# The mixed tile's column sums: written by ScalarE in row order to a gate buffer's free half, and read contiguously by the merge

## The reference, cut to what matters

```
def cross_scan(x):                       # x: image with 192 channels
    x0 = x.reshape(B, -1, L)             # position r*48+c  (row order)
    x1 = jnp.swapaxes(x, 2, 3).reshape(B, -1, L)   # position c*48+r  (column order)
    return jnp.stack([x0, x1, x0[..., ::-1], x1[..., ::-1]], axis=1)

def cross_merge(ys):
    y0 = ys[:, 0] + ys[:, 2][..., ::-1]
    y1 = ys[:, 1] + ys[:, 3][..., ::-1]
    y1 = jnp.swapaxes(y1.reshape(B, -1, W, H), 2, 3).reshape(B, -1, L)
    return y0 + y1                       # the column sums are turned to row order and added
```

## Time and profile before

| | |
|---|---|
| median of 3 runs | 26110.75 us (26106.58 to 26113.38) |
| the profiled execution | 26116.4 us, of which 26114.6 are the span of its instructions |
| PE busy | 24103.6 us (92%) |
| DVE busy | 24585.9 us (94%) |
| ACT busy | 22109.2 us (85%) |
| POOL busy | 20746.8 us (79%) |
| mean granted TensorE clock | 0.983 |

### The profile page before, as it was taken

How to read it: one execution, slowest core, us unless ns; L and a number is a source line. 1 busy time by engine, 2 the same in 40 slices (tenths; PEclk the granted TensorE clock), 3 DMA queues, 4 the chain that set the end, 5 groups by cost and what they waited for, 6 DMA issues and landing times.

```text
span 26114.6 us, 381945 instructions
## 1 busy us (share of the span) xinstructions
PE 24103.6 (92%) x95328; PEld 13330.2 (51%) x95328; DVE 24585.9 (94%) x17625; ACT 22109.2 (85%) x50283; POOL 20746.8 (79%) x11892
## 2 busy tenths in 40 slices
PE   8999999999999999999989999999999999999998
PEld 4555555555555555555545555555555555555554
DVE  9999999999999999999989999999999999999999
ACT  8888988889888888889878888888988888988888
POOL 7777977788777977778768987778987778977778
PEclk9999999999999999999999999999999999999999
DMA  4444544444444544445444544444544444544444
GB/s 155 132 135 132 172 133 133 133 149 154 133 136 132 169 135 134 135 139 164 129 125 144 164 154 145 146 145 144 171 148 144 145 146 143 173 145 145 147 144 149
DMA packets 1419233, 3790.03 MB, mean 145 GB/s; under 512 B 205888, under 2 KB 206016, under 8 KB 1416384
## 3 DMA queue, kind: packets, MB, share of 16 engines
q1 hardware_dynamic: 1416768, 3762.72, 46.1%
HBM read 3686.39 MB, written 47.19 MB: 143 GB/s over the span
## 4 chain that ended last, share of the span: by engine, by line
PE 29%; DVE 26%; issue 25%; ACT 13%; POOL 4%; DMA 2%; DVEq 1%; SPq 0%; ACTq 0%; POOLq 0%
DVE arena L1506 11%; PE ps L813 11%; DVE ps L1501 10%; ACT arena L1246 5%; POOL arena L1646 3%; ACT arena L1180 3%; DVE arena L572 3%; PE ps L691 3%; PE ps L781 3%; PE ps L1021 2%; DMA arena<-c_rows 2%; PE ps L801 2%; PE ps L653 1%; PE ps L638 1%; PE ps L823 1%
## 5 line engine op out<-in xcount | busy, mean ns | idle before, releaser
L1646 POOL TENSOR_TENSOR arena<-arena 128x768 f32<-128x768 f32 x9216 | 16574.4, 1825 | 1406.1 <-DVE arena L1506 1090.0
L813 PE MATMUL ps<-arena,consts 128*128 128x384 f32 x36864 | 13640.4, 493 | 183.8 <-ACT arena L1280 169.7
L1506 DVE TENSOR_TENSOR_SCAN arena<-arena,carry,ps 128x768 f32<-128x768 f32 x6144 | 10902.1, 1804 | 357.3 <-PE ps L781 198.5
L1180 ACT ACTIVATE arena<-arena,An 128x768 f32<-128x768 f32 x9216 | 8458.9, 930 | 1436.1 <-POOL arena L1646 1431.0
L813 PEld LDWEIGHTS ps<-arena,consts 128*128 128x128 f32 x36864 | 6313.1, 191 | 3951.2 <-issue 486.3
L1506 DVE TENSOR_TENSOR_SCAN arena<-arena,ps 128x768 f32<-128x768 f32 x3072 | 5273.0, 1745 | 264.4 <-PE ps L781 150.3
L1501 DVE TENSOR_TENSOR ps<-ps,arena 128x768 f32<-128x768 f32 x5600 | 5281.6, 943 | 160.0 <-PE ps L801 157.0
L781 PE MATMUL ps<-consts,arena 128*128 128x128 f32 x21696 | 3055.8, 277 | 946.3 <-DVE arena L1506 750.0
L1246 ACT ACTIVATE arena<-arena 128x64 f32<-128x64 f32 (+1 forms) x13824 | 3907.9, 365 | 20.3
L1246 ACT ACTIVATE arena<-arena,bT 128x64 f32<-128x64 f32 (+1 forms) x13440 | 3813.8, 367 | 20.4
L781 PEld LDWEIGHTS ps<-consts,arena 128*128 128x128 f32 x21696 | 2482.8, 141 | 2613.2 <-issue 1425.6
(11 more groups left out here) (180 smaller groups left out, 19274.6 us busy)
## 6 DMA issues: line engine op xcount, KB each, us to landing
arena<-c_rows SPq DMA_DIRECT2D x6144, 384.0 KB, 3.8
arena<-c_rows SPq DMA_DIRECT2D x6144, 192.0 KB, 3.6
arena<-x SPq DMA_DIRECT2D x32, 864.0 KB, 7.1
arena<-arena SPq DMA_DIRECT2D x384, 72.0 KB, 2.4
arena<-mid SPq DMA_DIRECT2D x32, 864.0 KB, 6.4
c_rows<-arena SPq DMA_DIRECT2D x96, 192.0 KB, 3.1
mid<-arena SPq DMA_DIRECT2D x16, 864.0 KB, 3.9
out<-arena SPq DMA_DIRECT2D x16, 864.0 KB, 3.9
```

The costliest lines, as they stand in the source:

```text
L813: mm = pe.matmul(y_part[:, h, :], ident, hC[it % NH][:, h * SEG:(h + 1) * SEG], start=(n == 0), stop=(n == NS - 1))
L1180: act.activation(state_at[it % NW], delta[g % 2], ACT.Exp, scale=An[:, slot(s) * NS + n:slot(s) * NS + n + 1]).then_inc(sem["da_ready"], 1)
L1506: dve.tensor_tensor_scan(a[:, ::back], a[:, ::back], slots[it % 2][:, ::back], 0.0 if k == 0 else carry[:, n:n + 1], ALU.mult, ALU.add).th ...
L1646: pool.tensor_tensor(hC[it % NH], state_at[it % NW], Csb[b], ALU.mult).then_inc(sem["hc_ready"], 1)
```

## The change

ACT's copy of the mixed tile's second pass (g = 3, 4, 5) becomes two copies: the lower 64 partitions go to `u[1]` as before; the upper 64 go to the upper 64 partitions of the gate buffer `sz[1]` (`y_rows`), and are written in row order, so that ACT's writes step by 48 elements. The semaphore `y_moved` is raised by the second copy. The merge's second matmul reads `y_rows` contiguously, from 64 partitions with a 64 x 64 identity in place of 128 partitions with a 128 x 64 one.

```diff
+        y_rows = arena[:, Y + 2 * L:Y + 3 * L]
+        lower, upper = slice(0, DB), slice(DB, P)
@@ merge_columns
-                    at, r = c * CH + h * SEG, (2 * c + h) * SEGROWS
+                    at = c * CH + h * SEG
                     pe.matmul(pre_part[0:DB, h, :], ident[:, 0:DB], u[1][:, at:at + SEG], start=True, stop=False)
-                    mm = pe.matmul(pre_part[0:DB, h, :], ident[:, DB:P], by_column(u[1])[:, r:r + SEGROWS, :],
-                                   start=False, stop=True)
+                    mm = pe.matmul(pre_part[0:DB, h, :], ident[DB:P, DB:P], y_rows[DB:P, at:at + SEG], start=False, stop=True)
@@ move_sums
-                act.copy(halves(chunk(ysum if p == 0 else u[j], c)), y_part).then_inc(sem["y_moved"], 1)
+                if p == 1 and j == 1:
+                    act.copy(halves(chunk(u[1], c))[lower, :, :], y_part[lower, :, :])
+                    cols = y_rows[upper, :].rearrange("p (r c) -> p c r", c=W)[:, 2 * c * SEGROWS:2 * (c + 1) * SEGROWS, :]
+                    act.copy(cols.rearrange("p (g c) r -> p g c r", g=2), y_part[upper, :, :].rearrange("p g (c r) -> p g c r", r=H))\
+                        .then_inc(sem["y_moved"], 1)
+                else:
+                    act.copy(halves(chunk(ysum if p == 0 else u[j], c)), y_part).then_inc(sem["y_moved"], 1)
```

## The result

The changed kernel takes 26158.21 us (median of 17 runs, 26145.28 to 26176.75) against 26113.0 before (17 runs, 26099.57 to 26122.14). The ratio is 1.0019, with a 95% interval from 1.0012 to 1.0026: 45 us slower, where 22 us faster was forecast. The profiled execution has a span of 26163.1 us, 48.5 more than before.

The account below looks back on a forecast made before the run. DVE was taken to bound the scan wherever it isn't made to wait. From the profiled 26116.4 us, minus 121 for the merges, plus 99 for the moves, gave 26094, or 26089 as a median; range 26022 to 26153.

Parts of the forecast that it names:

- What bounds the kernel: DVE sets the scan's pace wherever it isn't made to wait: busy 35.74 of 36.05 us in a plain group.
- The stride's price on both sides: PE's strided merge matmul 1.45 us against 0.76 contiguous; ScalarE's strided upper copy 1.47 us against 0.78.
- The delays: Moves 1.45 us late: group 4 pays 1.45, group 5 0.60, group 6 0.64 (layer 1) or 1.45 (layer 0); 99 us.
- The merge, 1.26 us: Groups 7 to 9: two contiguous matmuls a merge save 1.26 us of PE time, all on the path; 121 us.
- Group 4, 1.45 us: PE and DVE already wait for the move there, so the whole delay of 1.45 us a round is charged.
- the rival of the falling clock: Group 4: longer PE idling, 2.3 us, brings 1.2 GHz; 3.3 us a round, 106 us in all, 26195; chance 0.06.
- one wait of 1.53 us without a sequel: PE's idle time in group 2, after which matmuls kept their speed; idling of 4.15 us had slowed them.
- The sum: Merge gain of 121 us against move cost of 99 us: 26089 us, 0.08% less than before.
- the ScalarE rival: ScalarE bounds groups 4 to 6, so each move costs its full delay, 96 x 1.7 = 163 us: 26153; chance 0.09.

Follow-up runs that it names:

- the run with the clock held throughout: The changed kernel, with PE turning the product of iteration 4 of group 4 twice: 26121.05 us, ratio 1.0004 to the kernel before.
- the run of the merge alone: Kernel before, only the merge's second matmul reading u[1] contiguously, sums in column order: 128 partitions 25990.72 us (0.9955); 64 partitions 26034.69 us (0.9968).
- the late run: Kernel before, with ScalarE copying 1530 contiguous columns ahead of each of the three moves, the move still one copy: 26285.34 us, ratio 1.0066.

## Why the prediction was wrong

- **What bounds the kernel: right.** What groups 4 to 6 became longer and 7 to 9 shorter adds up to the change of the span within 8 us, at nearly unchanged busy time of DVE; the groups behind them kept their length.
- **The stride's price on both sides: right.** 508 ns for 502 on PE, 1.466 us for 1.47 on ACT.
- **The delays: right where the clock held.** Group 5 costs 20.7 us against 19, layer 1's group 6 11.0 against 10; group 4 costs 1.38 a round in the run with the clock held throughout, and 1.50 in the change's own rounds at 1.00, against 1.45. Layer 0's group 6 costs 28.4 against 23; there 8 rounds in place of 4 are at 0.92, and 4 more stretches of the lower clock at some 1.3 us each would be the 5 us.
- **The merge, 1.26 us: wrong, 0.86 (39 us in all).** The step was to put the contiguous pair beside it in the chain, 0.65 us, in the place of a matmul of another shape. That pair's weights had the shape of their neighbours', and with another shape beside them both kinds of pair take 0.785 us. The sum left the untouched matmul at its price, which rose by 0.22 us a merge. L1021's 0.76 us for 64 partitions is near to 0.785, but no help by itself: the difference of the two busy times, 1.45 - 0.76, would have made the gain larger still. With 128 partitions the 1.26 is had: 124 us in the run of the merge alone.
- **Group 4, 1.45 us: wrong, 2.45 (32 us in all).** The sum put the clock at nothing there. It was the rival of the falling clock, at a chance of 0.06 and with a cost of "about 2.3 us a round" as the point from which it decides. It came behind waits from 1.47 us up in group 4 (the longer ones didn't all bring it), and of 1.16 in group 5 of the late run. The error was to read a bound from one wait of 1.53 us without a sequel and to ask for more than that. A fall costs some 1.2 to 1.4 us here, not the 3.3 of my estimate. That came from a round at 0.92, as 4 of the 16 rounds of that group have it; most falls in group 4 are at 0.96, which over 40.4 us is 1.6 us of lost work. At 1.1 us a round on average the clock alone wouldn't have decided; 34 us on top of 26089 is 26123, within the range.
- **The sum.** Forecast -22, measured +56 over the touched groups; 39 of the 78 between are the weight loads, 32 group 4, the rest group 6 and rounding. The time fell 5 us outside the range. That its upper end came so close is luck: it was taken from the ScalarE rival, which charges every move its full delay, and group 5 (0.65 us for a delay of some 1.5) shows slack at work.

The sign hung on two terms that nearly cancel, 121 against 99. Each was 40 us off, both towards the slower side: 39 us of gain that didn't come, and 40 us of cost (32 in group 4, the rest in 5 and 6).

## What to carry to other kernels

A price that is moved to another engine is only gone if its new place has slack: the moves with the strided write cost 134 us with the merge unchanged where TensorE waits for them, while the same turning in another iteration, where ScalarE is idle anyway, costs next to nothing (25994 us, against 25991 for the merge alone over 128 partitions). Where TensorE waits longer than before, look at the granted clock of that stretch in many rounds, not in one, and put the rise of its instructions' time into the sum. Don't take it for granted that fewer partitions make a matmul cheaper: between neighbours of another shape it was the slower one here, and slowed them too.

## What the runs showed of the hardware

- Contiguous fp32 matmuls of 384 columns that alternate between 64 x 64 and 128 x 64 weights start every 0.785 us; with 128 x 64 weights throughout, the step between them is 0.65 to 0.70 us (runs of the merge alone).
- The granted clock fell to its lower level (1.2 GHz) within the busy scan, behind waits of PE of 1.16 to 1.18 us (14 of 32 rounds of group 5 in the late run) and 1.47 to 2.33 us (25 of 32 rounds of group 4 after the change). Waits as long had no sequel in other rounds of the same groups, nor had those of 1.03 us in group 5 after the change, or of 1.70 us in layer 1's group 6. Waiting time alone doesn't decide it; what PE did before differs between these places, and what of that counts stays open.
- Filling 0.8 us of such a wait with repeated matmuls made the kernel 37 us faster, and the clock held in all 32 rounds of group 4.
- ScalarE's copy of 64 x 768 fp32 out of PSUM takes 0.78 us contiguously and 1.466 us when its writes step by 192 bytes; TensorE's reading at that step takes 812 ns an instruction of 384 columns against 508 without it.
